# Decay product and mask of G moved from VectorE to GpSimd, and conv taps over two blocks, in the preparation of a Mamba-2 and MLP kernel

## The reference

```python
zxbcdt = hidden_states @ W_in
z = zxbcdt[..., :D_INNER]
xbc = zxbcdt[..., D_INNER:D_INNER + CONV_DIM]
dt = zxbcdt[..., D_INNER + CONV_DIM:]
xbc = _causal_conv1d(xbc, conv_w, conv_b)      # four taps, then silu
...
dt = jax.nn.softplus(dt + dt_bias)
dA = dt * A                                    # the decay product
dA_cs = jnp.cumsum(dA)                         # its running sum
G[j, i] = B[j] . C[i], kept where i >= j       # the mask
y = sum_j G[j, i] * exp(dA_cs[i] - dA_cs[j]) * dt[j] * x[j]  + D * x
out = rms_norm(y * silu(z)) * norm_w @ W_out
```

## Time and profile before

| | us |
|---|---|
| median of 3 runs | 1493.66 |
| lowest and highest | 1489.96, 1496.38 |
| the profiled execution | 1488.68 |
| its span | 1486.9 |
| end of `prepare` (last silu of z) | 72.75 |

### The profile page before, as it was taken

How to read it: one execution, slowest core, us unless ns; L and a number is a source line. 1 busy time by engine, 2 the same in 40 slices (tenths; PEclk the granted TensorE clock), 3 DMA queues, 4 the chain that set the end, 5 groups by cost and what they waited for, 6 DMA issues and landing times. The chain is left out here.

```text
span 1486.9 us, 27692 instructions
## 1 busy us (share of the span) xinstructions
PE 1424.6 (96%) x9432; PEld 1198.3 (81%) x9432; DVE 1237.1 (83%) x2380; ACT 1126.7 (76%) x2020; POOL 1064.4 (72%) x731
## 2 busy tenths in 40 slices
PE   6679999999999999999999988999999999999998
PEld 5557877878788788778787767999998989989988
DVE  6899999999999999999999982567677676776662
ACT  5689999999999999999999974566564555645542
POOL 4379999999999999999999995635263352634550
PEclk9999999999999999999999998999999999999999
DMA  4223232332323232323323222201002010020011
GB/s 145 71 93 122 72 121 79 103 105 93 107 97 109 67 133 74 110 91 100 107 93 107 75 75 90 68 1 47 23 1 67 0 38 29 0 81 0 1 58 42
DMA packets 50160, 107.63 MB, mean 72 GB/s; under 512 B 13248, under 2 KB 25792, under 8 KB 48448
## 3 DMA queue, kind: packets, MB, share of 16 engines
q1 hardware_dynamic: 50048, 106.21, 22.0%
HBM read 101.47 MB, written 4.72 MB: 71 GB/s over the span
## 5 line engine op out<-in xcount | busy, mean ns | idle before, releaser
L1438 DVE TENSOR_TENSOR mlp_hlo<-mlp_h,mlp_hhi 128x512 fp32r<-128x512 f32 x192 | 218.1, 1138 | 175.8 <-ACT mlp_hhi L1370 175.6
L1365 ACT ACTIVATE mlp_h<-mlp_p,mlp_b1c 128x512 f32<-128x512 f32 x192 | 131.9, 687 | 202.8 <-PE mlp_p L501 197.0
L687 POOL TENSOR_TENSOR mix_dec<-mix_dec,gmat 128x768 f32<-128x768 f32 x151 | 278.1, 1856 | 10.4 <-ACT mix_dec L884 6.8
L517 DVE SCALAR_TENSOR_TENSOR xt<-mix_pab,conv,xt 128x1020 f32<-128x1020 f32 x186 | 236.2, 1270 | 12.7 <-ACT xt L856 9.2
L1331 PE MATMUL mlp_p<-mlp_w2hi,mlp_hhi 128*128 128x256 f32 x768 | 218.4, 284 | 2.6 <-DVE acc L1497 2.6
L1333 PE MATMUL mlp_p<-mlp_w2hi,mlp_hlo 128*128 128x256 f32 x768 | 216.3, 282 | 0.0
L1012 DVE SCALAR_TENSOR_TENSOR mix_dec<-srow,tokpar,mix_floor 128x128 f32<-128x128 f32 (+1 forms) x688 | 214.2, 373 | 1.9 <-PE mix_py L778 1.9
L1332 PE MATMUL mlp_p<-mlp_w2lo,mlp_hhi 128*128 128x256 f32 x768 | 215.8, 281 | 0.0
L501 PE MATMUL mix_pab<-xhi,whi 128*128 128x512 f32 x496 | 206.0, 415 | 2.0 <-DVE xt L517 0.2
L501 PE MATMUL mix_pab<-xlo,whi 128*128 128x512 f32 x496 | 196.5, 396 | 0.0
L501 PE MATMUL mix_pab<-xhi,wlo 128*128 128x512 f32 x496 | 196.5, 396 | 0.0
(11 more groups left out here) (141 smaller groups left out, 3646.6 us busy)
## 6 DMA issues: line engine op xcount, KB each, us to landing
srow<-cs_rows SPq DMA_DIRECT2D x128, 512.0 KB, 4.6
wraw<-w_xz SPq DMA_DIRECT2D x32, 256.0 KB, 5.1
w1raw<-w SPq DMA_DIRECT2D x6, 1028.0 KB, 4.8
mlp_w2raw<-w SPq DMA_DIRECT2D x6, 1024.0 KB, 6.7
mix_oraw<-w_out SPq DMA_DIRECT2D x16, 257.0 KB, 2.7
prep_hid<-hidden SPq DMA_DIRECT2D x4, 512.0 KB, 6.5
xn_rows<-prep_hid SPq DMA_DIRECT2D x4, 512.0 KB, 2.9
mlp_res<-xn_rows SPq DMA_DIRECT2D x1, 2048.0 KB, 10.8
```

The costliest lines, as they stand in the source:

```text
L517: return dve.scalar_tensor_tensor(d[:, :, k:SEQ], s[:, :, 0:SEQ - k], weight, d[:, :, k:SEQ], ALU.mult, ALU.add)
L687: pool.tensor_tensor(d, d, g, ALU.mult).then_inc(pool_g_done, 1)
L1438: dve.tensor_tensor(hlo[:, j, :], h[:, j % 4, :], hhi[:, j, :].bitcast(F32), ALU.subtract).then_inc(hlo_done, 1)
```

## The change

- The decay product moves from VectorE to GpSimd. It was a `tensor_scalar` with two multiplications over 64 partitions x 512; it is now the same over all 128 partitions, after each block's softplus sum. VectorE keeps the running sums (`sums(b)`).
- The mask of G moves from VectorE to GpSimd. ScalarE copies G from PSUM to `gmat` unmasked (`copy_g`), and GpSimd multiplies in place (`mask_g`). TensorE's g(s) now waits for the copy of s - 2, not for its mask.
- `taps` and `first_taps` do two blocks in one instruction (128 x 4 x 255 in place of twice 128 x 2 x 255); the eight PSUM banks become one tensor, so that two neighbours can be addressed together. Both blocks' `conv_done` now rise at the end of the pair.
- On VectorE, the running sums of blocks 0 and 1 come before `taps(2)`, those of blocks 2 and 3 before `taps(3)`.

```diff
+        banks = ctx.enter_context(nc.psum_tensor("prep_banks", [P, 8 * BLK], F32))
+        bank = [banks[:, i * BLK:(i + 1) * BLK] for i in range(8)]
...
@@ gpsimd
                 pool.tensor_tensor(u[:, c], v[:, c], u[:, c], ALU.add
                                    ).then_inc(softplus_done, 1)
+                pool.wait_ge(softplus_done, b + 1)
+                pool.tensor_scalar(v[:, c], u[:, c], par[:, 1:2], -1.0, ALU.mult,
+                                   ALU.mult).then_inc(decay_done, 1)
+            def mask_g(s):
+                pool.wait_ge(g_copied, s + 1)
+                pool.tensor_tensor(gmat[:, s, :], gmat[:, s, :], mask[:], ALU.mult).then_inc(g_masked, 1)
+
+            for s in range(4):
+                mask_g(s)
             for b in range(NB):
                 ...
+            for s in range(4, NSEQ):
+                mask_g(s)
@@ tensor, g(s)
                 if s >= 2:
-                    pe.wait_ge(g_masked, s - 1)
+                    pe.wait_ge(g_copied, s - 1)
@@ scalar
+            def copy_g(s):
+                act.wait_ge(g_done, s + 1)
+                act.copy(gmat[:, s, :], bank[4 + s % 2][:, 0:LW]).then_inc(g_copied, 1)
...
                 act.activation(c, c, ACT.Silu).then_inc(bct_done, 1)
+                if n in (NB + 1, NB + 3):
+                    copy_g(n - NB - 1)
+                    copy_g(n - NB)
...
                 act.activation(x, x, ACT.Silu).then_inc(stages.x_done, 1)
+                if b % 2 == 0:
+                    copy_g(4 + b)
+                    copy_g(5 + b)
@@ vector, taps(pair)
+                m, b = 2 * pair // NB, 2 * pair % NB
+                first = (NB + 2 * pair) % 8
                 for k in range(1, TAPS):
-                    for i in range(2):
...
+                    conv_tap(dve, bct[:, m, b * BLK:(b + 2) * BLK],
+                             banks[:, first * BLK:(first + 2) * BLK],
+                             cbc[:, m, TAPS - 1 - k:TAPS - k], k
+                             ).then_inc(tap_done if k < TAPS - 1 else conv_done, 2)
@@ vector, order
             taps(0)
             taps(1)
+            sums(0)
+            sums(1)
             taps(2)
-            decays(0)
-            decays(1)
+            sums(2)
+            sums(3)
             taps(3)
-            masked_g(0)
-            masked_g(1)
-            decays(2)
-            decays(3)
             first_taps(0)
-            masked_g(2)
-            masked_g(3)
             first_taps(1)
-            for s in range(4, NSEQ):
-                masked_g(s)
```

More of the change, by code:

```diff
@@ L138, in prepare @@
         tiny = sb("tiny", [P, 1])
-        bank = [ctx.enter_context(nc.psum_tensor(f"prep_bank{i}", [P, BLK], F32)) for i in range(8)]
+        banks = ctx.enter_context(nc.psum_tensor("prep_banks", [P, 8 * BLK], F32))
+        bank = [banks[:, i * BLK:(i + 1) * BLK] for i in range(8)]
         tp = [bank[4:6], bank[6:8]]
@@ L180, in prepare @@
         g_done = sem("g_done")
+        g_copied = sem("g_copied")
         g_masked = sem("g_masked")
@@ L338, in _ @@
                     act.wait_ge(xt_done, KD * b + k + 1)
-                    act.copy(xhi[:, k, b * BLK:(b + 1) * BLK], tp[b % 2][k][:]).then_inc(hi_done, 1)
+                    act.copy(xhi[:, k, b * BLK:(b + 1) * BLK], tp[b % 2][k]).then_inc(hi_done, 1)
             for c in range(2):
@@ L416, in taps, with sums @@
             def taps(pair):
+                m, b = 2 * pair // NB, 2 * pair % NB
+                first = (NB + 2 * pair) % 8
                 for k in range(1, TAPS):
-                    for i in range(2):
-                        n = 2 * pair + i
-                        m, b = n // NB, n % NB
-                        if k == 1:
-                            dve.wait_ge(conv0_done, n + 1)
-                        else:
-                            dve.wait_ge(tap_done, 4 * pair + 2 * (k - 2) + i + 1)
-                        conv_tap(dve, bct[:, m, b * BLK:(b + 1) * BLK], bank[(NB + n) % 8][:],
-                                 cbc[:, m, TAPS - 1 - k:TAPS - k], k
-                                 ).then_inc(tap_done if k < TAPS - 1 else conv_done, 1)
-            def decays(b):
-                c = slice(b * BLK, (b + 1) * BLK)
-                dve.wait_ge(softplus_done, b + 1)
-                dve.tensor_scalar(v[HD:P, c], u[HD:P, c], par[HD:P, 1:2], -1.0, ALU.mult,
-                                  ALU.mult).then_inc(decay_done, 1)
+                    if k == 1:
+                        dve.wait_ge(conv0_done, 2 * pair + 2)
+                    else:
+                        dve.wait_ge(tap_done, 4 * pair + 2 * (k - 1))
+                    conv_tap(dve, bct[:, m, b * BLK:(b + 2) * BLK],
+                             banks[:, first * BLK:(first + 2) * BLK],
+                             cbc[:, m, TAPS - 1 - k:TAPS - k], k
+                             ).then_inc(tap_done if k < TAPS - 1 else conv_done, 2)
+            def sums(b):
                 dve.wait_ge(decay_done, b + 1)
@@ L446, in first_taps @@
                 done = [stages.conv0_done, stages.tap1_done, stages.tap2_done, stages.conv_done]
+                b, first = 2 * pair, (6, 0)[pair]
                 for k in range(1, TAPS):
-                    for b in (2 * pair, 2 * pair + 1):
-                        dve.wait_ge(done[k - 1], b + 1)
-                        conv_tap(dve, xt[:, 0, b * BLK:(b + 1) * BLK], bank[(6, 7, 0, 1)[b]][:],
-                                 conv[:, 0, TAPS - 1 - k:TAPS - k], k).then_inc(done[k], 1)
-            def masked_g(s):
-                dve.wait_ge(g_done, s + 1)
-                dve.tensor_tensor(gmat[:, s, :], bank[4 + s % 2][:, 0:LW], mask[:],
-                                  ALU.mult).then_inc(g_masked, 1)
+                    dve.wait_ge(done[k - 1], b + 2)
+                    conv_tap(dve, xt[:, 0, b * BLK:(b + 2) * BLK],
+                             banks[:, first * BLK:(first + 2) * BLK],
+                             conv[:, 0, TAPS - 1 - k:TAPS - k], k).then_inc(done[k], 2)
             moments(0)
```

20 lines of the change are left out of this document (11 added, 9 removed).

## The result

| | before | after |
|---|---|---|
| median, us (20 executions each) | 1489.99 | 1497.45 |
| lowest and highest | 1488.45, 1496.71 | 1494.55, 1504.11 |
| span of the profiled execution | 1486.9 | 1495.4 |
| end of `prepare` (last silu of z) | 72.75 | 78.85 |

The ratio is 1.0053, 95% interval 1.0043 to 1.0064: slower by about half a per cent, on the edge of what I had called the same. The measured time lies in the range on record, but the predicted effect was +0.7 us and the measured one is +7.5. `prepare` alone ends 6.1 us later; forecast were 0.7. So the number was near only because 0.7 and 7.5 are both small against 1490, and because the median of three that it was added to (1493.66) lies 3.7 us above the median of twenty: from 1489.99 on, the same forecast would have been 1490.7.

A forecast was written before the change was run, and what follows sets the result against it. Two chains were taken to bound TensorE's g(4): VectorE's mask of G, ending last, and silu of C, Ln, transposes. Mask wait -2.85 and later Ln +3.5 gave +0.7 us on 1493.66: 1494.4, range 1489 to 1500.

The forecast's parts named there:

- Mask wait, -2.85: TensorE's 2.85 us wait for VectorE's mask of G, ahead of g(4), was to vanish.
- Pairing, 0.0: VectorE's taps over two blocks: three double taps take 3.95 us, six single ones 3.93, so no gain.
- rival of the instruction count: VectorE: each double tap saves a fixed 0.16 us on two single ones; total 1493.9 down to 1491.4; chance 0.04.
- Product, 1.28: GpSimd's decay product takes 1.28 us per block; the fourth makes VectorE wait 1.1 us before block 3's sums.
- Sums of two blocks 2 x 1.2: VectorE's running sums of blocks 0 and 1, ahead of `taps(2)`, take 1.2 us a block, ending at 43.8.
- x groups "1.4 each": TensorE's x projections of blocks 2 and 3 start at 47.8, after `taps(2)`, and take 1.4 us each.
- That cover is 1 us wide: ScalarE's first two silus and copies of G end at 54.2, within its wait for `taps(3)`, with 1 us to spare.
- Loads of `srow`, 6 us earlier at no gain: SyncE gets the sums, and so issues its loads, 6 us earlier; nobody waited for them, so 0.
- Transposes 3.46: TensorE's transposes of the sums and their copies take 3.46 us as before, ending at 62.7.
- The final chain: TensorE from g(4) to the last z projection, 10.7 us before: same work and same lower-clock time, left equal.
- TensorE stays at its lower clock: Rival: three more z projections and the G's at the lower clock add about 4.5 us; total 1498.9; chance 0.08.
- GpSimd becomes the bound: Rival: a product of 2.5 us on GpSimd makes g(4) 5.6 us late; total 1499.3; chance 0.06.

The follow-up runs named there:

- e7: The changed kernel with taps over one block each, as before; product, masks and order stay; median 1499.67 us, ratio to before 1.0057.
- e6: The changed kernel with the scans' factor of ones read from a PSUM bank in place of SBUF; median 1492.65 us, ratio to before 1.0019.
- e3: The changed kernel with 54 matmuls whose result nobody reads in TensorE's three idle gaps; median 1494.52 us, ratio to before 1.0023.
- e1: The changed kernel with GpSimd's softplus block 2 held until VectorE's first four scans are done; median 1498.41 us, ratio to before 1.0055.
- e5: The changed kernel with GpSimd waiting for the first four scans and unread matmuls (16, 13, 15) in TensorE's gaps; median 1494.62 us, ratio to before 1.0021.
- e2: The changed kernel with VectorE's running sums back in their old places; product, masks and double taps stay; median 1492.83 us, ratio to before 1.0018.
- e4: The kernel before with only G copied by ScalarE and masked on GpSimd; median 1490.88 us, ratio to before 1.0015.
- e11: e8 without the filling matmuls on TensorE; median 1488.04 us, ratio to before 0.9981.
- e12: The kernel before with only the decay product of the four blocks moved to GpSimd; median 1491.44 us, ratio to before 1.0003.
- e8: The kernel before with G copied by ScalarE (2, 3 later), masked on GpSimd after all running sums, and filling matmuls on TensorE; median 1488.21 us, ratio 0.9982.
- e10: e8 with VectorE's last product of w1 and G in mix's last tile given to GpSimd; median 1486.93 us, ratio to before 0.9975.

## Why the prediction was right or wrong

The number is in its range and the mechanism is not the one forecast. That it is in the range is luck: the cases behind the range reached from -4.0 to +5.6 us, the effect is +7.5, and the base of the sum was 3.7 too high. Step by step, measured against forecast:

- **Mask wait, -2.85: right.** g(4) starts without a wait, behind the transposes.
- **Pairing, 0.0: right** (3.95 forecast, 4.04 and 4.02 measured, double and single). The rival of the instruction count is refuted by e7.
- **Copies of G, 0.4 each: right** (0.85 for two back to back). Masks of about 1.0: right (3.95 for four).
- **Product, 1.28: wrong.** It takes 0.69, and VectorE does not wait before the sums of block 3 (1.1 forecast). The lower bound of 0.44 was nearer, and so was the estimate of 0.44 us and overhead that the prediction drew from the Trainium skill, GPSIMD Engine Reference, "Performance versus the Vector engine". This error went in the change's favour, and its gain was eaten by the next.
- **"Sums of two blocks 2 x 1.2": the step that failed first.** I priced the scans by rows in which GpSimd had already ended: the earlier trace rows have them from 45.91 on, GpSimd's last sum was over at 44.53 (its row, from the timeline of GpSimd before, stands under this point). The new order puts the scans at 41.9, beside GpSimd, and the products keep it busy some 3 us longer (to 47.73 in e6, where nobody is slowed, and to 49.35 in after). Measured 5.56 instead of 2.4, +3.2.

```profile
43.25 1.28 POOL L240 TENSOR_TENSOR prep_u<-prep_v,prep_u 128x512 f32<-128x512 f32 x1
```

- **x groups "1.4 each": wrong by the clock.** 2.56 each at the lower level, +2.3. I had left the clock equal for the final chain and had not asked what it would be behind TensorE's wait for `taps(2)`. e3 gives the 1.40 back, and so do e1 and e6.
- **"That cover is 1 us wide": right in size, overrun.** Start +0.4, scans +3.2, small gaps 0.2, x groups +2.3 and another 0.3 make 6.4; less 1.05 of cover, the Ln starts 5.3 later than forecast (63.70, forecast 58.4).
- **Loads of `srow`, 6 us earlier at no gain: half right.** SyncE issues them at 58.34, 3.35 (not 6) earlier than in the earlier trace rows, and nobody waited for them before or after.
- **Transposes 3.46: 4.08 measured** (64.52 to 68.60), +0.6, the clock again. **The final chain** was 0.45 shorter than before, as it ran mostly at the upper level. Together: 73.4 + 5.3 + 0.6 - 0.45 = 78.85, which is what was measured.

Of the rivals, "TensorE stays at its lower clock" held in kind, but at other places than named, x groups and transposes and not z, and priced the whole effect at +5.2 us. "GpSimd becomes the bound" was the right engine with the wrong mechanism: not VectorE waiting for a product, but both engines in each other's way. Its price (+5.6 us) was passed with a product of half the estimated length. The chance of 0.04 for slower was too low, since no rival held any cost of two engines side by side.

What is shown and what is not: that the scans' two SBUF inputs beside GpSimd are the cause of their slowness is shown by e6 and, from the other side, by e1. That the lower clock costs some 4 us in after is shown by e3. In the medians e6 gives back 4.8 of the 7.5 us and e3 2.9, and both cures together (e5) 2.8; which of the two counts for more in the whole time stays open. Smaller gains at the end of `prepare` (e2 -1.7, e4 -1.3) did not arrive in the medians, and I can't say where they went; the groups of executions and a varying `mlp` (579.8 to 588.7 us behind `mix` in the fourteen traces, with the same code there) hide it.

## What to carry to other kernels

Before work is moved to GpSimd, look at what VectorE does in the same microseconds: an instruction of its with two inputs from SBUF is slowed beside a busy GpSimd (and one with a single tensor input can be, as the product in e4), and its row in the trace of before shows the price only if GpSimd was busy there. If a scan must stand there, put one input in PSUM. And price a delay of TensorE with what it does to its clock: here 3.2 us of slow scans brought 2.3 more at the lower level.

## What the runs showed of the hardware

- A scan of 64x256 on VectorE with both inputs in SBUF: 0.6 us in a row of four alone (2.44), 1.4 beside GpSimd (5.56); with one input in PSUM 0.6 beside it too (2.47). Taps, with one input in PSUM, took their usual time beside GpSimd (4.04 in after). A `tensor_scalar` of 64x512 with one tensor input from SBUF did not: 1.15 us beside the masks of e4, 0.47 alone.
- GpSimd pays as well: 1.27 to 1.65 for two inputs of 128x512, 0.69 to 0.95 for a `tensor_scalar`, 1.85 to 2.56 for 128x768.
- The contest can end in starvation: 9.66 us for an instruction of 1.86, in e5, e6, e11 and e12 (9.63 to 9.66), through five rows of GpSimd's instructions without a gap. In these four traces `mix` took 812.7 to 814.1 us, in the ten others 807.3 to 809.7. The Trainium skill, SBUF — State Buffer, section "Who interferes with whom", says of the port pair that VectorE and GpSimd share that it is an exclusive lock, which whoever issues first has for the whole instruction (said there of VectorE's 2-port modes) while the other blocks; by that VectorE would have had its turn at the end of GpSimd's running instruction, at 882.1. It ended at 890.65, 0.8 behind the end of GpSimd's whole run. Here the trace differs from the page, and the trace decides.
- TensorE's clock fell to the lower of its levels (granted clock 0.54 to 0.57 over whole stretches) behind waits of 1.8 us (in e12) to 5.2 us (in e6), not behind each of them (in e6 the first eight transposes behind a wait of 2.98 us still took 1.29), and in e3, e5, e8 and e10 matmuls whose result nobody reads kept it at 1.00.
